# Part of the transposes of w taken from TensorE by way of DRAM and VectorE, x + ctx moved from VectorE to ScalarE and GpSimd, and the first w taken in contiguous halves

## The reference

```python
# block 1, per sample: inp_q = layernorm(x), inp_v = inp_k = ctx
t, p, g = Wt @ ctx, Wp @ layernorm(x), Wg @ ctx
att = sum over group and columns of p * g          # 8 groups of 32 rows
y = Wz (grouped) @ (att * t)
y = groupnorm(y) * gn_w + gn_b + ctx
w = x + tanh(g_xattn) * y
# block 2, per sample
h = layernorm(w)
z = h @ A_w.T                                      # 512 columns: 64 experts of rank 8
gate = softmax of the 16 largest of 64 router scores, 0 elsewhere
out = w + tanh(g_ffn) * 2 * ((z * gate) @ B_w.T)
```

## Time and profile before

| what | value |
|---|---|
| median of 3 runs | 340.39 us (338.96 to 341.2) |
| the profiled execution, own time | 341.37 us |
| its span, first to last instruction | 339.6 us, so 1.77 us lie around it |
| mean granted TensorE clock | 0.989 |

### The profile page before, as it was taken

One profiled execution on the slowest core, in us unless ns is written; L12 is line 12 of the kernel. 1 busy time (PEld: TensorE's weight loads), 2 busy tenths in 40 slices (PEclk: granted clock), 3 DMA queues, 4 the chain that ended last, 5 costly groups with the idle time before them and its releaser, 6 DMA issues.

```text
span 339.6 us, 5620 instructions
## 1 busy us (share of the span) xinstructions
PE 331.7 (98%) x2024; PEld 298.8 (88%) x2024; DVE 246.2 (73%) x625; ACT 161.6 (48%) x286; POOL 162.5 (48%) x146
## 2 busy tenths in 40 slices
PE   8999999999999999899999999999999999999996
PEld 6588898899988998788999899898999899989984
DVE  0866996684779879678797697867897785773462
ACT  2596835684374453375516662183535632342310
POOL 0173798199158599055940859036860620010000
PEclk9998999999999999799999999999999999999999
DMA  7999702960912574159521874238621121103002
GB/s 252 409 388 398 279 2 55 353 212 5 322 46 93 182 284 124 31 162 299 194 72 26 245 280 154 62 108 296 234 77 33 32 92 41 54 3 124 2 31 93
DMA packets 21227, 52.21 MB, mean 154 GB/s; under 512 B 2112, under 2 KB 6848, under 8 KB 21200
## 3 DMA queue, kind: packets, MB, share of 16 engines
q1 hardware_dynamic: 20848, 51.65, 44.2%
q10 hardware_dynamic: 352, 0.20, 0.2%
HBM read 41.10 MB, written 10.75 MB: 153 GB/s over the span
## 4 chain that ended last, share of the span: by engine, by line
PE 85%; DVE 8%; POOL 4%; issue 2%; DVEq 0%; POOLq 0%
PE w_ps L1205 16%; PE z_ps L1175 16%; PE w_ps L1091 10%; PE w_ps L1175 9%; PE w_ps L1212 8%; PE z_ps L1042 7%; PE z_ps L1021 4%; PE t_ps L1152 3%; PE w_ps L1069 2%; PE w_ps L1042 2%; PE t_ps L1119 2%; POOL c_lo L365 1%; DVE x_st L706 1%; POOL A_lo L353 1%; PE w_ps L1219 1%
## 5 line engine op out<-in xcount | busy, mean ns | idle before, releaser
L1205 PE MATMUL w_ps<-B_hi,zT_hi 128*128 128x512 f32 x128 | 51.9, 406 | 0.0
L1205 PE MATMUL w_ps<-B_lo,zT_hi 128*128 128x512 f32 x128 | 50.2, 392 | 0.0
L346 POOL TENSOR_TENSOR xT_lo<-xT_in,xT_hi 128x512 fp32r<-128x512 f32 x24 | 35.5, 1498 | 22.0 <-ACT xT_hi L458 19.2
L389 POOL TENSOR_TENSOR y_rs<-y_ve,minus_half 128x2 f32<-128x2 f32 x8 | 5.9, 742 | 71.4 <-DVE y_ve L789 71.4
L365 POOL TENSOR_TENSOR c_lo<-c_sb,c_hi 128x512 fp32r<-128x512 f32 x24 | 30.3, 1303 | 11.7 <-DVE uw L811 11.7
L346 POOL TENSOR_TENSOR cT_lo<-cT_in,cT_hi 128x512 fp32r<-128x512 f32 x24 | 35.5, 1500 | 0.0
L1175 PE MATMUL z_ps<-A_hi,hT_hi 128*128 128x288 f32 x160 | 34.7, 298 | 0.3 <-POOL A_lo L353 0.3
L1212 PE MATMUL w_ps<-B_hi,zT_lo 128*128 128x512 f32 x128 | 34.5, 391 | 0.0
L508 ACT ACTIVATE uw<-w_ps,neg_u 128x512 f32<-128x512 f32 x32 | 20.1, 684 | 30.2 <-DVE neg_u L756 30.2
L1175 PE MATMUL z_ps<-A_lo,hT_hi 128*128 128x288 f32 x160 | 34.1, 295 | 0.0
L525 ACT ACTIVATE hT_hi<-t_ps 128x512 fp32r<-128x512 f32 x32 | 17.5, 595 | 27.9 <-PE t_ps L1152 27.3
(11 more groups left out here) (164 smaller groups left out, 860.7 us busy)
## 6 DMA issues: line engine op xcount, KB each, us to landing
c_sb<-in_ctx SPq DMA_DIRECT2D x16, 512.0 KB, 5.5
x_sb<-in_x SPq DMA_DIRECT2D x16, 512.0 KB, 5.2
xT_in<-in_xT SPq DMA_DIRECT2D x14, 512.0 KB, 7.8
cT_in<-in_cT SPq DMA_DIRECT2D x14, 512.0 KB, 9.1
out_block<-uw SPq DMA_DIRECT2D x14, 512.0 KB, 4.3
z_through<-zg_sb SPq DMA_DIRECT2D x9, 256.0 KB, 2.3
products<-z_through SPq DMA_DIRECT2D x9, 256.0 KB, 2.7
A_in<-in_aT SPq DMA_DIRECT2D x8, 256.0 KB, 12.4
```

The costliest lines, as they stand in the source:

```text
L346: last = pool.tensor_tensor(lo[:, chunks, :], came[:, chunks, :], hi[:, chunks, :].bitcast(f32), ALU.subtract)
L1205: pe.matmul(w_ps[k][:, :], zT_hi[:, t, row], w[:, j, cols], start=(j == 0 and w is B_hi), stop=False)
```

## The change

1. w of samples 3 to 6 (`turned_h`) is no longer transposed on PE: SP writes each tile of w to DRAM (`write_w`, 512 KB), reads it back into the c_sb tile that w has just been made from (`read_w`), and DVE transposes it into t_ps with two instructions of 128x512 per tile (`hT_turn`), then splits as before. Samples 0, 1, 2 and 7 stay on PE.
2. x + ctx of samples 3 to 7: ACT's `scale_ctx(m + 1)` at the end of a pass and POOL's `x_add(m + 1)` at the head of its own next pass, in place of POOL's x_shift and DVE's x_plus_ctx.
3. SP's order: load_x(m + 2) and load_c(m + 2) between the two stores at the end, behind x_add(m + 1) and behind hT_done; load_transposes(m + 2) behind the four DMAs of w.
4. ACT: xT_high and cT_high of the second half behind exps(0). DVE: zT_low(0) between the two w tiles, minus_means behind zT_low(1).
5. first_w takes contiguous halves, hT(t, 0) waits for both halves of its tile; group_means(2) no longer waits for att_rows.

```diff
+        w_through = nc.dram_tensor("w_through", (T, 4 * P * (D // 4)), f32).ap()
+        w_scratch, z_scratch = (a.rearrange("t (i p d) -> t p i d", i=4, p=P) for a in (w_through, z_through))
+        w_rows, z_rows = (a.rearrange("t (q d) -> t q d", q=P) for a in (w_through, z_through))
+        def turned_h(n):
+            return 3 <= n < NB - 1
...
             def load_c(n):
                 for t in range(T):
-                    if n > 1:
+                    if n > 1 and turned_h(n - 2):
+                        sp.wait_ge(hT_done, per_use(n - 2, NH * t + 1))
+                    elif n > 1:
                         sp.wait_ge(w_done, per_tile(n - 2, t))
...
+            def write_w(t, n):
+                sp.wait_ge(w_done, per_tile(n, t))
+                sp.dma_start(w_scratch[t], uw[n % 2][:, t, :].rearrange("p (i d) -> p i d", i=4)).then_inc(w_out[t], 16)
+            def read_w(t, n):
+                sp.wait_ge(w_out[t], 16 * (n - 2))
+                sp.dma_start(c_sb[n % 2][:, t, :], w_rows[t]).then_inc(w_back[t], 16)
...
-                if m + 1 < NB:
+                if b == 2:
                     load_x(m + 1)
                 for t in range(T):
                     if turned_z(t, b):
                         write_z(t, b)
                         read_z(t, b)
+                if turned_h(m):
+                    for t in range(T):
+                        write_w(t, m)
+                    for t in range(T):
+                        read_w(t, m)
                 if m + 2 < NB:
-                    load_c(m + 2)
                     load_transposes(m + 2)
                 store(b, 0)
+                if m + 2 < NB:
+                    load_x(m + 2)
+                    load_c(m + 2)
                 store(b, 1)
...
             def x_add(n):
                 for t in range(T):
-                    pool.wait_ge(c_scaled, per_tile(n, t))
+                    pool.wait_ge(c_scaled, per_tile(n if n < 2 else n - 1, t))
...
-            x_shift(3)
             for m in range(3, NB):
+                x_add(m)
...
                 w_root(m)
-                if m + 1 < NB:
-                    x_shift(m + 1)
...
+            scale_ctx(3)
             for b in range(2, NB - 1):
                 m = b + 1
                 if m + 1 < NB:
-                    transposes_high(m + 1)
+                    xT_high(0, m + 1)
+                    cT_high(0, m + 1)
                 exps(0, b)
+                if m + 1 < NB:
+                    xT_high(1, m + 1)
+                    cT_high(1, m + 1)
                 residual(b)
...
                     M_high(m + 1)
+                    scale_ctx(m + 1)
                 hT_high(0, m)
                 hT_high(1, m)
...
             def first_w(k):
-                t, g = divmod(k, NH)
-                rows, sums = (parts(a[0][:, t, :])[:, g * KH:(g + 1) * KH, :] for a in (uw, c_sb))
-                dve.wait_ge(u_copied, per_use(0, NH * t + NH - 1))
+                t, cols = use(k)
+                dve.wait_ge(u_copied, per_use(0, k))
                 dve.wait_ge(xt_done, per_tile(0, t))
...
+            def hT_turn(t, n):
+                dve.wait_ge(w_back[t], 16 * (n - 2))
+                rows = c_sb[n % 2][:, t, :].rearrange("p (g c j) -> p g j c", g=4, c=32)
+                for g in range(NH):
+                    if t > 0:
+                        dve.wait_ge(hT_lo_s, per_use(n, g))
+                    elif g == 0:
+                        dve.wait_ge(zT_lo_s, per_tile(n - 1, T - 1))
+                    else:
+                        dve.wait_ge(va_read, n + 1)
+                    dve.transpose(t_ps[g][:, :].rearrange("p (j r g) -> p g j r", j=4, g=4),
+                                  rows[:, :, g * 4:g * 4 + 4, :]).then_inc(hT_done, 1)
+                hT_low(t, n)
...
             for b in range(2, NB - 1):
                 m = b + 1
-                x_plus_ctx(m)
                 gate(0, b)
...
                 slopes(m, lambda: zT_turn(0, b))
-                w_tiles(m)
+                w_tiles(m, (0,))
                 zT_low(0, b)
+                w_tiles(m, (1,))
                 if b < NB - 2:
-                    minus_means(m + 1)
                     zT_turn(1, b)
                     zT_low(1, b)
+                    minus_means(m + 1)
...
-                    hT_low(0, m)
+                    hT_turn(0, m)
                     add_out(2, b)
-                    hT_low(1, m)
+                    hT_turn(1, m)
                     add_out(3, b)
...
             def group_means(n):
-                if n >= 2:
+                if n >= 3:
                     pe.wait_ge(att_rows, per_tile(n, T - 1))
...
             def hT(t, n):
                 for g in range(2):
-                    if n == 0 and g == 0:
-                        pe.wait_ge(w_half, t + 1)
-                    else:
-                        pe.wait_ge(w_done, per_tile(n, t))
+                    pe.wait_ge(w_done, per_tile(n, t))
...
-                    out_product(2, b, {2: lambda: hT(0, m)})
-                    out_product(3, b, {2: lambda: hT(1, m)})
+                    out_product(2, b)
+                    out_product(3, b)
```

More of the change, by code:

```diff
@@ L74, in flamingo_block @@
         stage = sb("stage", [P, D + NE])
+        w_through = nc.dram_tensor("w_through", (T, 4 * P * (D // 4)), f32).ap()
         z_through = nc.dram_tensor("z_through", (T, 4 * P * (NN // 4)), f32).ap()
-        z_scratch = z_through.rearrange("t (i p d) -> t p i d", i=4, p=P)
-        z_rows = z_through.rearrange("t (q d) -> t q d", q=P)
+        w_scratch, z_scratch = (a.rearrange("t (i p d) -> t p i d", i=4, p=P) for a in (w_through, z_through))
+        w_rows, z_rows = (a.rearrange("t (q d) -> t q d", q=P) for a in (w_through, z_through))
         ident, group_mean = sb("ident", [P, P]), sb("group_mean", [P, P])
@@ L168, in flamingo_block @@
         kappa0_done, w_half = sem("kappa0_done"), sem("w_half")
-        z_out, z_back = sems("z_out", T), sems("z_back", T)
+        w_out, w_back, z_out, z_back = sems("w_out", T), sems("w_back", T), sems("z_out", T), sems("z_back", T)
         block = stack.enter_context(nc.Block())
@@ L617, in _ @@
             offsets(1)
[L618 to L621, removed]
             for t in range(T):
@@ L698, in x_plus_ctx @@
                 for t in range(T):
-                    dve.wait_ge(x_shifted, per_tile(n - 2, t))
+                    dve.wait_ge(x_shifted, t + 1)
                     dve.scalar_tensor_tensor(c_sb[n % 2][:, t, :], c_sb[n % 2][:, t, :], tg[:, 0:1], x_sb[:, t, :],
@@ L798, in first_w, with w_tiles @@
             def first_w(k):
-                t, g = divmod(k, NH)
-                rows, sums = (parts(a[0][:, t, :])[:, g * KH:(g + 1) * KH, :] for a in (uw, c_sb))
-                dve.wait_ge(u_copied, per_use(0, NH * t + NH - 1))
+                t, cols = use(k)
+                dve.wait_ge(u_copied, per_use(0, k))
                 dve.wait_ge(xt_done, per_tile(0, t))
[L804 to L808, removed]
+                last = dve.scalar_tensor_tensor(uw[0][:, t, cols], uw[0][:, t, cols], slope[:, t:t + 1],
+                                                c_sb[0][:, t, cols], ALU.mult, ALU.add)
+                last.then_inc(w_done if k % NH == NH - 1 else w_half, 1)
+            def w_tiles(n, tiles=range(T)):
+                for t in tiles:
                     dve.wait_ge(u_copied, u_use(n, NH * t + NH - 1))
```

## The result

The changed kernel takes 335.69 us (median of 10 runs, 334.36 to 337.49) against 339.13 for the kernel before (10 runs). The ratio is 0.9871 with a 95% interval of 0.9844 to 0.9898, so 4.4 us faster by the ratio, between 3.5 and 5.3. The medians are 3.4 us apart and the means 4.1: six of the ten runs of the kernel before lie between 338.8 and 339.2 us, the other four between 340.4 and 342.0, and a median says little of two such groups. So the ratio is the measure here.

A forecast was written before the change was run, and what follows sets the result against it. PE was taken as the bound, busy 331.7 of 339.6 us. Terms -7.1 + 1.5 - 0.3 - 0.5 = -6.4 us from the profiled 341.37 gave 335.0, then 334.0 for the median lying 0.98 lower; 8-in-10 range 330.8 to 339.5.

The forecast's parts named there:

- the narrower forecast: The whole kernel's time between 332.5 and 336.5 us, given a chance of 0.58.
- first w: At the head, w is whole 0.9 us earlier, so A_lo's 0.34 us wait on PE goes: -0.3 us.
- group_means(2) without its wait: PE's wait of 0.57 us for att_var goes: -0.5 us taken.
- Transposes off PE: In passes 2 to 5, 1.77 us per pass comes off PE's path: 7.1 us in all.
- The way by DRAM fits: Write and read of w take 7 to 8 us, back at offset 33 to 34, before DVE needs it: cost 0.
- The seam rival: Slow turns or late w make z_product(0, m) wait, giving back the gain: 336.5 to 340 us, chance 0.17.
- x + ctx hidden on ACT and POOL: scale_ctx, POOL's adds and the load of x stay hidden at the pass seam, with 1 to 2 us of cover.
- 0.5 us a pass, 3 x 0.5 = 1.5 us: In passes 3 to 5, POOL's later subtractions slow x_ve and neg_x; PE stands 0.2 to 0.8 us at zg of tile 1.
- 0; ends -3.7 and +1: In pass 2, the 1.88 us stop at zg of tile 1 and its clock fall stay: 0, bounds -3.7 and +1 us.
- Slower by gate(1) over 3 us late: Late load_transposes delays gate(0), x_stats and gate(1), so PE stops in passes 3 to 5: 347 us, chance 0.07.
- the signs named: 64 fewer PE transposes, passes 3 to 5 37.2 to 37.9 us, no head idle, zg stops 0.2 to 0.8, neg_x 1.2 or more.

The follow-up runs named there:

- narrow moments: The changed kernel with x_ve and neg_x written as four 128x1 operations in place of two 128x2: 330.29 us, ratio 0.9688 to the kernel before.
- the run with another order: The changed kernel with read_w put behind load_transposes in SP's order: 354.74 us, ratio 1.0441 to the kernel before.
- the kernel with the move alone: The changed kernel with w of samples 3 to 6 transposed by TensorE again, x + ctx staying on ScalarE and GpSimd: 342.43 us, ratio 1.0036 to before.
- the head-only kernel: The kernel before with only first w in contiguous halves and group_means(2) without its wait: 338.91 us, ratio 0.9947 to the kernel before.
- the run with the turn only: The changed kernel with w's way by DRAM kept but x + ctx back on VectorE: 350.13 us, ratio 1.0258 to the kernel before.

## Why the prediction was right, and by how much it was off

334.0 us was predicted, 335.69 measured, inside the range of 330.8 to 339.5 and inside the narrower forecast. The time looks nearer than the gain was: 6.4 us of gain were predicted and 4.4 measured, and the interval of 3.5 to 5.3 doesn't reach 6.4. The prediction was set off from a median of 340.39 us, and the kernel before then ran at 339.13, which hid part of the miss. The mechanism of each part came, and the sizes were off. Step by step, start to start in the two traces, without the 1.7 us of clock in the head:

| step | predicted us | measured us |
|---|---|---|
| first w | -0.3 | -0.8 |
| group_means(2) without its wait | -0.5 | -0.7 |
| pass 2 | -1.8 (transposes), stop unchanged | -0.9 |
| passes 3 to 5 | -5.3 + 1.5 | -2.6 |
| sum | -6.4 | -5.0, and -4.4 in the timed runs |

The passes gave 2.1 us less than predicted and the head 0.7 us more, so that the sum came as near as it did is in part luck.

- *Transposes off PE: right, slightly under.* 1.77 us a pass was predicted from the pieces of the chain. With nothing else late a pass went from 38.97 to 37.02 us (narrow moments): 1.95 us, since the matmuls around the transposes also close up.
- *The way by DRAM fits: right.* 7 to 8 us was taken, the medians are 3.2 + 4.1 = 7.3. The estimate of 3.2 us for each DMA fits the writes; the reads took 3.3 to 4.7. DVE came to hT_turn in pass 4 at offset 230.64 - 195.06 = 35.6, for 35.0 predicted. A turn takes 1.17 us, against 1.1 taken and up to 1.8 bounded: a stride of 8 columns costs hardly more than the 1.13 us of the turns of z with one of 4. The seam rival was the right one to fear all the same; the run with another order shows it at 19 us. Its price was too mild, though: from its own terms, 340.4 less 0.8 and less 0 to 1.2 us in each of four passes, it comes to 334.8 to 339.6 and not to 336.5 to 340, so it overlapped with the forecast.
- *x + ctx hidden on ACT and POOL: right*, since no adds and no scale_ctx are in the chain of passes 3 to 5. That the move helps by itself, as I had read from x_plus_ctx's 4.16 us, doesn't show: made alone it loses. And with the move and the turns came the largest loss. This is the term "0.5 us a pass, 3 x 0.5 = 1.5 us", whose mechanism (x_ve and neg_x beside POOL's subtractions) came as described, with the subtractions from 5.7 to 15.8 us into pass 4. It was mis-sized. I took both together as 1.2 to 1.6 us longer; they took 2.17 us (207.43 to 209.60) where they took 0.24, so 1.9 longer. PE stood 0.69 to 0.88 us, and a stop costs some 0.3 us beyond the idle time in brackets, which I had not counted. Together passes 3 to 5 are 1.0 to 1.2 us longer than the 37.02 of the narrow moments, 3.2 us in all for the 1.5.
- *Pass 2: the side of the bound.* "0; ends -3.7 and +1": the stop grew by 1.05 us, the worse end. The load of x(4) was issued 1 us later, as worked out, but DVE's timeline shows tile 1 of x_stats waiting 2.08 us for it: it landed after 3.9 us, not after the 3.2 of the earlier trace rows. That DVE begins gate(0) earlier, on which I had leaned, bought nothing, since x_stats now waits for that load where it had not waited before. The chain goes there by scale_ctx (1.25 us), the adds (5.07) and the load (3.94).
- *The head: too low.* I had counted only the 0.34 us of idle time for A_lo. Start to start (39.92 to 40.69, where such matmuls follow at 0.27) it cost 0.5, and the transposes of tile 1 held the next matmuls for 1.08 us before and 0.81 after.
- *Slower by gate(1) over 3 us late* did not come: xT_high and cT_high of the first half were done at 201.6 and exps(0) ran at 202.3, in time.

Of the signs named, most came: 64 transposes fewer, 16 turns, no idle time at the pass heads, neg_x at 1.33 us, each DMA of w in 3.0 to 4.7 us, a granted clock of 1.00 all through passes 3 to 6. Two were just missed, both by the mis-sized term: the passes are 37.98 to 38.20 us long, over the 37.2 to 37.9, and one stop is 0.88, over the 0.8.

The 5.2 us of the two traces lie inside the interval of the timed runs, at its upper end.

What stays open: why passes 3 to 5 of the kernel with the move alone are 0.4 us longer, each in the second transposes of w (1.28 for 0.88 us in the chain) and in u_product's second half (2.90 for 2.75); no run took these apart.

## What to carry to other kernels

When work is moved to another engine, ask what else moves in time with it, and whose small operations now run beside that: here the adds of a pass were hidden, but POOL's old subtractions came later, and two operations on two columns each, in lines that the change doesn't touch, cost some 6 us, more than the 4.4 us that the whole change gained. A pair of parts can lose when each is made alone (3.1% and 0.9% of the time, against the head-only kernel) and win together, so they have to be tried together, and each one's cost read from the engine that has to make room. And a DMA that something waits for belongs ahead of bulk loads on its queue: the place in the order was worth 19 us over three passes, when the reads of w came back after 9.2 to 9.6 us instead of 3.3 to 4.7.

## What the hardware showed that I had not expected

- An operation of VectorE on 128x2 float32 in SBUF (tensor_scalar) ended only when the GpSimd subtraction beside it did, 1.33 us for 0.16. On 128x1 the same operation takes 0.14 to 0.15 us beside the same GpSimd instructions. The Trainium skill (SBUF — State Buffer, section Who interferes with whom) has the first half, an exclusive lock for a whole instruction, and the traces agree to 0.05 us; that a width of one column gets around it is shown by the run with the narrow moments.
- TensorE's granted clock stayed at 1.00 after stops of 0.57 to 1.22 us in these profiles, and fell to the 1.2 GHz level after those of 1.88 and 2.93 us in the two kernels, of 3.9 in the run with the turn only and of 4.7 to 5.5 in the one with the reads behind the loads. It also fell where there was no stop at all: in the kernel before PE was busy for all of the eight microseconds from 20 to 28, and the clock was 1.00 in the first four and 0.60 in the next.
- A stop costs PE more than the idle time that the profile gives it, even at full clock. In pass 4 twelve matmuls from one start to the next piece's take 2.86 us behind the stop (212.71 to 215.57) and 2.74 without one (216.72 to 219.46 before); the rest of the 0.3 us is the overlap of neighbouring matmuls, which a stop breaks: in the chain the same twelve count 3.02 and 2.75.
